# A two-layer graph attention network and expert layer on one core: one more buffer, and the order of the work between the layers

## The reference

```python
x = layernorm(x) -> graph network -> + x;   then layernorm -> expert layer -> + x     # 3125 x 256
def _gat(x, src, dst, W, a_src, a_dst, b, heads, ch, concat):
    h = (x @ W).reshape(n, heads, ch)
    es = (h * a_src).sum(-1); ed = (h * a_dst).sum(-1)
    e = leaky_relu(es[src] + ed[dst], 0.2)
    w = exp(e - segment_max(e, dst)[dst])
    out = segment_sum(h[src] * (w / segment_sum(w, dst)[dst])[:, :, None], dst)
h = _gat(x, ..., heads=4, ch=64, concat=True)      # layer 1
h = relu(_layernorm(h, ln_g, ln_b))
out = _gat(h, ..., heads=1, ch=256, concat=False)  # layer 2
```

## Time and profile before

| | |
|---|---|
| median of 3 runs | 1420.41 us (1419.89 to 1422.87) |
| the profiled execution: its own time, its span | 1427.7 us, 1426.0 us |
| TensorE busy | 1182.3 us, 83% |
| VectorE, ScalarE, GpSimd busy | 858.3, 689.4, 700.6 us (60%, 48%, 49%) |
| mean granted TensorE clock | 0.936 of full speed |
| layer 1, steps | about 84 to 613 us of the span |
| between the layers | about 613 to 640 us |
| layer 2, steps | about 640 to 971 us |
| expert layer | the rest |

### The profile page before, as it was taken

The page is one execution under the profiler, slowest core; times in us unless marked ns, Lnnn a source line. Parts: engine busy times, 40 slices in busy tenths (PEclk is TensorE's granted clock), DMA queues, the critical chain, the costliest instruction groups (busy, mean ns, idle before and its releaser), DMA issues.

```text
span 1426.0 us, 24459 instructions
## 1 busy us (share of the span) xinstructions
PE 1182.3 (83%) x7697; PEld 819.6 (57%) x7698; DVE 858.3 (60%) x2544; ACT 689.4 (48%) x1833; POOL 700.6 (49%) x621
## 2 busy tenths in 40 slices
PE   2765998879888889957787888783799999999997
PEld 1654333334333433435465565552799999999996
DVE  8778988788789778743476765787422222222222
ACT  1567676657566666733333433340534344334432
POOL 1002778557668663017676666630244445454544
PEclk9979999999999999978898998996899999999999
DMA  7023633634643372053445554534033332323221
GB/s 248 1 73 123 168 103 105 181 96 110 168 128 103 108 190 67 27 210 110 151 139 178 168 178 123 181 99 108 12 98 96 94 95 40 92 37 97 35 37 27
DMA packets 137151, 157.04 MB, mean 110 GB/s; under 512 B 58935, under 2 KB 116504, under 8 KB 137064
## 3 DMA queue, kind: packets, MB, share of 16 engines
q0 software_dynamic: 33616, 73.02, 20.9%
q1 hardware_dynamic: 101344, 81.57, 18.6%
q10 hardware_dynamic: 2104, 1.38, 0.3%
HBM read 121.19 MB, written 35.52 MB: 110 GB/s over the span
## 4 chain that ended last, share of the span: by engine, by line
PE 42%; DVE 21%; ACT 9%; issue 9%; another core or an unknown queue 6%; DMA 5%; POOL 5%; ACTq 1%; POOLq 0%; DVEq 0%; SPq 0%
PE bank L1449 11%; PE bank L1457 11%; PE bank L1321 6%; ACT ring_a L1042 5%; PE bank L1400 4%; POOL arena L801 4%; DVE ring_a L1937 3%; DVE ohk L1665 3%; DVE ohs L1661 2%; PE bank L1277 2%; DMA out_x<-ring_a,si 2%; PE bank L1370 1%; DVE st L1546 1%; ACT XE L1006 1%
## 5 line engine op out<-in xcount | busy, mean ns | idle before, releaser
L801 POOL DMA_INDIRECT arena<-rows,idx_e x365 | 405.3, 1110 | 321.0 <-issue 92.2
L1321 PE MATMUL bank<-ring_a,slots 128*65 128x384 f32 (+1 forms) x1000 | 356.6, 465 | 34.2 <-DVE ring_a L1937 28.5
L1042 ACT ACTIVATE ring_a<-vbb,slots 128x384 f32<-128x384 f32 (+1 forms) x500 | 243.8, 562 | 16.2 <-DMA vbb<-v_rows 7.6
L1400 PE MATMUL bank<-h2t,ring_a 128*128 128x257 f32 x700 | 187.9, 412 | 32.8 <-issue 16.8
L1937 DVE SCALAR_TENSOR_TENSOR ring_a<-ring_a,arena 128x1536 f32<-128x1536 f32 (+1 forms) x125 | 192.7, 1543 | 31.2 <-ACT ring_a L1042 23.5
L1150 ACT ACTIVATE ring_a<-bank,cols 128x128 f32<-128x128 f32 x432 | 128.6, 370 | 160.1 <-PE bank L1449 159.6
L1321 PEld LDWEIGHTS bank<-ring_a,slots 128*65 128x65 f32 x1000 | 127.6, 144 | 112.5 <-issue 57.2
L1400 PEld LDWEIGHTS bank<-h2t,ring_a 128*128 128x128 f32 x700 | 136.8, 205 | 68.2 <-issue 25.4
L1449 PEld LDWEIGHTS bank<-ring_a,arena 128*128 128x128 f32 x1056 | 123.1, 192 | 1.7
L1449 PE MATMUL bank<-ring_a,arena 128*128 128x128 f32 x1056 | 123.2, 275 | 0.0
L847 POOL DMA_INDIRECT gs<-gates,gk x54 | 51.2, 949 | 146.2 <-DVE gk L2089 137.6
(11 more groups left out here) (303 smaller groups left out, 1644.5 us busy)
## 6 DMA issues: line engine op xcount, KB each, us to landing
counts_all<-arena SPq DMA_DIRECT2D x14, 800.0 KB
arena<-counts_all SPq DMA_DIRECT2D x14, 800.0 KB
arena<-in_L_ffn_W SPq DMA_DIRECT2D x8, 1024.0 KB, 7.5
vbb<-v_pairs SPq DMA_DIRECT2D x23, 320.0 KB
arena<-rows,idx_e POOLq DMA_INDIRECT x365
XB<-general_sums SPq DMA_DIRECT2D x38, 130.0 KB
vbb<-in_L_ffn_W SPq DMA_DIRECT2D x4, 1024.0 KB
spare<-in_L_ffn_W SPq DMA_DIRECT2D x4, 1024.0 KB
```

Of the source, the lines that this page charges most:

```text
L801: pool.indirect_dma_start(to[:, k, 0:width], None, table, bass.IndirectOffsetOnAxis(idx_e[:, m * PAIR + k:m * PAIR + k + 1], 0)).then_inc( ...
L1042: ins = act.activation(S1[q % SLOTS1][:, h * k * P:(h + 1) * k * P].rearrange("p (t n) -> p t n", n=P), vb1[:, 0:k, h, :], ACT.Copy, scale ...
L1321: pe.matmul(bank[h][0:CH + 1, 0:w_], slots[:, s, h * (CH + 1):(h + 1) * (CH + 1)], S1[q % SLOTS1][:, h * w_:(h + 1) * w_], start=(s == 0), ...
L1400: ins = pe.matmul(bank[(j % 2) * 2 + i][:, 0:W2T], S2[q2 % SLOTS2][:, i * P:(i + 1) * P], h2t[:, s, 0:W2T], start=(s == 0), stop=(s == NT ...
```

## The change

Five edits, made together. (1) `PAIR2` starts at step 8 rather than 3 and ends at 162 rather than 163. The pairs of pairs are then used at steps 11, 19, 26, 34, 41, 49 and so on to 162. (2) The last dense block of layer 1 makes three groups of one tile each, with spreads at 126, 128, 130 and norms at 129, 131, 133 as before; roots at 130, 132, 134, refinements at 131, 133, 135 and turns at 133, 135, 137. (3) Block 0 of layer 1 has a buffer of its own, `vb0`, and `block_rows(1)` goes out ahead of the 25 stores of the first table, with no wait on s_r. (4) `np2` is made by ScalarE instead of VectorE, and VectorE no longer waits for the second layer's exponentials. (5) The spread of layer 2's first scores and its copy (`spread_rows`, `rows_out`) stand ahead of the wait for the flags and the branch, and TensorE's spread waits for the first exponential (s_ex 3) instead of s_vt; ScalarE's wait for s_vt is gone.

```diff
-PAIR2 = [3 + p * 164 // PAIRS2 for p in range(PAIRS2)]
+PAIR2 = [8 + p * 158 // PAIRS2 for p in range(PAIRS2)]
...
-    groups = [Group(range(t0, t0 + k), True, NT * (b + 1)) for b, (t0, k) in enumerate(B1)]
+    groups = [Group(range(t0, t0 + k), True, NT * (b + 1)) for b, (t0, k) in enumerate(B1[:-1])]
+    groups += [Group([B1[-1][0] + i], True, NT * len(B1), 2 * i) for i in range(B1[-1][1])]
...
-        g.spread = [g.end + 1 + 2 * i for i in range(n)] if g.dense else []
+        g.spread = [g.end + 1 + g.late + 2 * i for i in range(n)] if g.dense else []
...
+        vb0 = sb("vb0", [P, B1[0][1], HEADS, P])
...
-                sp.wait_ge(s_r, b * NT)
+                if b > 1:
+                    sp.wait_ge(s_r, b * NT)
...
             half_tile_rows(1)
+            block_rows(1)
             for t in range(NT):
                 sp.wait_ge(s_scl, t + 1)
...
-                if q % NT == 0 and 0 < q // NT < len(B1):
+                if q % NT == 0 and 1 < q // NT < len(B1):
                     block_rows(q // NT)
...
                 act.activation(second, esm, ACT.Exp, scale=power).then_inc(s_ex, 1)
+                if layer:
+                    act.wait_ge(s_ex, 4)
+                    act.activation(np2[:, :, :], p2[:, :, :], ACT.Copy, scale=-1.0).then_inc(s_ex, 1)
...
-                act.activation(vb1[:, t, :, :], bank[7][:, :].rearrange("p (h n) -> p h n", h=HEADS), ACT.Copy).then_inc(s_vbs, 1)
+                act.activation(vb0[:, t, :, :], bank[7][:, :].rearrange("p (h n) -> p h n", h=HEADS), ACT.Copy).then_inc(s_vbs, 1)
...
-                                             vb1[:, 0:k, h, :], ACT.Copy, scale=u1[:, s, h:h + 1])
+                                             (vb1 if b else vb0)[:, 0:k, h, :], ACT.Copy, scale=u1[:, s, h:h + 1])
...
             weights(1, p2, pu2[:, :, :], v2, np2[:, :, :], v2[:, :, :], SLOPE)
+            rows_out(B1[0][1])
             act.wait_ge(s_fl, 2)
...
             act.sem_inc(s_gen, 1)
-            act.wait_ge(s_vt, 2)
...
             extremes(1, 1)
+            pe.wait_ge(s_ex, 3)
+            spread_rows(range(B2[0][0], B2[0][0] + B2[0][1]))
             pe.wait_ge(s_fl, 2)
...
             pe.wait_ge(s_vt, 2)
-            spread_rows(range(B2[0][0], B2[0][0] + B2[0][1]))
...
-                v.wait_ge(s_ex, 2 * layer + 2)
-                if layer:
-                    link(v.tensor_scalar(npv[:, :, :], p[:, :, :], -1.0, None, ALU.mult))
+                if layer == 0:
+                    v.wait_ge(s_ex, 2)
```

More of the change, by code:

```diff
@@ L141, with __init__ @@
 class Group:
-    def __init__(self, tiles, dense, end):
-        self.tiles, self.dense, self.end = list(tiles), dense, end
+    def __init__(self, tiles, dense, end, late=0):
+        self.tiles, self.dense, self.end, self.late = list(tiles), dense, end, late
 def plan1():
-    groups = [Group(range(t0, t0 + k), True, NT * (b + 1)) for b, (t0, k) in enumerate(B1)]
+    groups = [Group(range(t0, t0 + k), True, NT * (b + 1)) for b, (t0, k) in enumerate(B1[:-1])]
+    groups += [Group([B1[-1][0] + i], True, NT * len(B1), 2 * i) for i in range(B1[-1][1])]
     for t in range(NE, NT, 2):
@@ L1064, in _, with rows_out @@
                 q += 1
+            def rows_out(n):
+                act.wait_ge(s_vb, n + 1)
+                what = next((what for q, what in ROWS_AT.items() if ROWS_OF[q] == n), 0)
+                if isinstance(what, str):
+                    k = int(what[-1])
+                    m = len(EDGE_TILES[k * 4:k * 4 + 4]) * P
+                    act.activation(ve2[:, k * 512:k * 512 + m], bank[7][:, 0:m], ACT.Copy).then_inc(s_vbs, 1)
+                else:
+                    m = B2[what][1] * P
+                    act.activation(vb2[what % 2][:, 0:m], bank[7][:, 0:m], ACT.Copy).then_inc(s_vbs, 1)
             weights(1, p2, pu2[:, :, :], v2, np2[:, :, :], v2[:, :, :], SLOPE)
+            rows_out(B1[0][1])
             act.wait_ge(s_fl, 2)
@@ L1092, in hooks2 @@
                     act.activation(xnT[:, e % 4, :, :], bank[6][:, 0:D].rearrange("p (k n) -> p k n", k=2), ACT.Copy).then_inc(s_TS, 1)
-            def rows_out(n):
-                act.wait_ge(s_vb, n + 1)
-                what = next((what for q, what in ROWS_AT.items() if ROWS_OF[q] == n), 0)
-                if isinstance(what, str):
-                    k = int(what[-1])
-                    m = len(EDGE_TILES[k * 4:k * 4 + 4]) * P
-                    act.activation(ve2[:, k * 512:k * 512 + m], bank[7][:, 0:m], ACT.Copy).then_inc(s_vbs, 1)
-                else:
-                    m = B2[what][1] * P
-                    act.activation(vb2[what % 2][:, 0:m], bank[7][:, 0:m], ACT.Copy).then_inc(s_vbs, 1)
             def exponents(p):
@@ L1287, in hooks1 @@
                     for h in range(HEADS):
-                        ins = pe.transpose(bank[6][:, h * (CH + 1):(h + 1) * (CH + 1)], OT[0:CH + 1, h, i * P:(i + 1) * P],
+                        ins = pe.transpose(bank[6][:, h * (CH + 1):(h + 1) * (CH + 1)], OT[0:CH + 1, h, (t - CB[block_of(t)][0]) * P:(t - CB[block_of(t)][0] + 1) * P],
                                            ident[0:CH + 1, 0:CH + 1])
@@ L1334, in _, with spread_rows @@
                 q += 1
+            def spread_rows(tiles):
+                for i, t in enumerate(tiles):
+                    ins = pe.matmul(bank[7][:, i * P:(i + 1) * P], v2[:, t, 0:1].broadcast_to([P, P]), ident[:, :], start=True, stop=True)
+                ins.then_inc(s_vb, 1)
             pe.wait_ge(s_HS, 2 * NT)
@@ L1345, in _ @@
                 general_layer(1, 1, lambda s, h: h2t[:, s, 0:W2T], W2T)
-            def spread_rows(tiles):
-                for i, t in enumerate(tiles):
-                    ins = pe.matmul(bank[7][:, i * P:(i + 1) * P], v2[:, t, 0:1].broadcast_to([P, P]), ident[:, :], start=True, stop=True)
-                ins.then_inc(s_vb, 1)
             def rows_at(q):
@@ L1890, in hooks1 @@
                         X = XB[:, t % 2, ds(bad1, 1), :]
-                        o, s_done = orow[:, i, :], s_on
+                        o, s_done = orow[:, t - CB[block_of(t)][0], :], s_on
                     else:
@@ L1914, in hooks1 @@
                     after(v, s_T, NT + e - 3)
-                    o = orow[:, i, :] if g.dense else orow[:, edge_row(t), :]
+                    o = orow[:, t - CB[block_of(t)][0], :] if g.dense else orow[:, edge_row(t), :]
                     v.tensor_scalar(xn[:, e % 4, :], o, mv[:, t, 0:1], rstd[:, t:t + 1], ALU.subtract, ALU.mult).then_inc(s_xn, 1)
```

1 line of the change is left out of this document (removed).

## The result

The change made the kernel slower. On the chip of the comparison it took 1436.14 us (median of 20 runs, 1427.9 to 1444.6) against 1422.91 us for the kernel before (20 runs, 1417.57 to 1438.76): ratio **1.0084**, 95% interval 1.0066 to 1.0102. I had predicted 1417.2 us, three microseconds faster; the result is outside my range.

What follows compares the result with a forecast made beforehand. No engine was full throughout; layer 2 was taken as nearest to bound by GpSimd's gathers. Terms -4.9 - 0.2 + 0.9 + 1.0 gave -3.2 us, off the median 1420.41 to 1417.2 us, range 1411 to 1423.

Steps and rivals of the forecast that it cites:

- Own buffer, -4.9: Start of layer 1's block 1: ScalarE starts 6.4 us earlier, 1.5 lost waiting for gathers; -4.9 us, bounds -6.4 and -3.2.
- pair 0 ready: Start of block 1: pair 0, wanted at 143.1 us rather than 149.51, would have its gathered data by then.
- the 2.76 us from issue to use: A gather's data is usable 2.76 us after issue; used to put layer 1's pair 1 ready at 148.5 us.
- Rival C: Layer 1: the buffer's gain is waited off at several early pairs; +1.7 us, 1422.1 us; chance 0.13.
- rival E: Layer 1's first ten gathers: one or two slowed by busy VectorE; sum -1.5 us, 1418.9 us; chance 0.12.
- Three groups, -0.2: Between the layers: tiles 10 to 12 normalised singly, last store 0.2 us earlier; bounds -0.5 and +0.8.
- Spread ahead of the branches: Start of layer 2: first step 1.3 us earlier, hidden behind gathers already running, counted only as TensorE's lead.
- Pairs from step 8, +0.9: Layer 2, pairs 4 and 5: product delayed 4.7 us, less 1.3 and two thirds of 3.79 regained; +0.9 us.
- tail, +1.0: End of layer 2: 13 steps instead of 12 behind the last products; +1.18 or 0 if hidden, taken as +1.0 us.
- the gathers come nearest to setting layer 2's length: Layer 2: earlier work counts only if it starts the gathers earlier or shortens what follows the last one.
- 1.18 for the step: Layer 2's end: cost of one dense step, from 12 steps and hooks between 956.72 and 970.89 us.
- Rival D: Layer 2: TensorE late at pairs 4 and 5, product 6.1 us later; sum +2.8 us, 1423.2 us; chance 0.15.

Runs made afterwards that it cites:

- e18: Changed kernel with PAIR2 put back to steps 3 to 163, second time, on another even chip, against the kernel before: 0.9981.
- e17: Kernel before with only PAIR2 changed, to steps 8 to 162, second time, on another even chip: 1.0020.
- e3: Kernel before with only block 0's own score buffer and the early load of block 1, even chip: 1362.51 us, 0.9996.
- e12: Kernel before with own buffer, np2 on ScalarE, early spread, one group as before, and PAIR2 from 3 to 157, even chip: 1.0086.
- e11: Kernel before with only PAIR2 changed, to steps 3 to 157, even chip: 1.0070.
- e2: Changed kernel with PAIR2 put back to steps 3 to 163, even chip, against the kernel before: 1361.43 us, 0.9989.
- e4: Kernel before with only the last block's three groups of one tile, even chip: 1363.85 us, 0.9999.
- e1: Kernel before with only PAIR2 changed, to steps 8 to 162, even chip: 1368.28 us, 1.0034.
- e7: Kernel before with six slots instead of four for layer 2's pairs, pausing chip: 1452.29 us, 1.0104.
- e8: Kernel before with only PAIR2 changed, to steps 13 to 162, pausing chip: 1443.85 us, 1.0061.
- e14: Kernel before with only PAIR2 changed, to steps 8 to 167, pausing chip: 1.0042.
- e13: Kernel before with only PAIR2 changed, to steps 3 to 167, pausing chip: 1.0039.
- e16: Kernel before with only PAIR2 changed, to steps 3 to 162, pausing chip: 1.0017.
- e9: Kernel before, unaltered, run against itself on an even chip: 1.0006.
- e5: Changed kernel, unaltered, against the kernel before on a pausing chip: 1443.54 us, 1.0054.
- e15: Kernel before with own buffer, np2 on ScalarE, early spread, one group as before, and PAIR2 from 3 to 167, pausing chip: 0.9990.

## Why the prediction was wrong

*Own buffer, -4.9.* Right in mechanism. Layer 1's steps end 3.9 us earlier in the recorded pair and 4.0 between e18 and e17; the changed kernel's first dense matmul is 1.4 us later in the recorded pair, so the steps themselves are 5.4 shorter. ScalarE's and VectorE's waits went as worked out. The price was mis-sized: I had pair 0 ready, and it costs 1.69 us beside the 1.06 of pair 1. The reason is the 2.76 us from issue to use, which I took from layer 2: here the fifth gather is issued at 140.77 and its data used at 146.34, 5.57 us, and for pair 1 it is 3.61. All eight kernels with the buffer show both waits, 1.5 to 1.8 and 0.7 to 1.1 us; none of the twelve without it does. Rival C, that the gain is absorbed at early pairs, is seen too: in e3 and e12 VectorE waits another 2.6 and 2.7 us for gathered rows near 212 us, 6.1 in all, and e12's layer 1 is as long as e11's (500.4 and 500.1 us from its first matmul to its last) although block 1 starts 51.7 us behind the first step and not 57.7. In e2 and e18 these waits are under 0.5, and the layer takes 495.6 and 495.5. What decides between the two is open.

*The early gathers beside a busy VectorE (rival E).* I had read no price in the rows, and there is one. The first nine intervals of gathers took 14.15 us against 12.91, with one gather of 2.39. Over all traces it is 13.62 to 14.23 us in the eight kernels with the buffer, where VectorE is busy for 11.3 us or more of them, and 12.86 to 13.00 in the twelve without it, where it is busy for about 6: 0.6 to 1.4 us more. The direction is that of the Trainium skill's rule (SBUF — State Buffer, Who interferes with whom), which says that VectorE in a two-port mode keeps GpSimd out of the shared port. Whether VectorE's instructions here are of that mode, no run shows.

*Three groups, -0.2.* Measured +2.0 from layer 1's end to the first gather in the recorded pair, of which the slow projections are 1.5 (6.05 us against 4.52). The granted clock of the stretch is 0.56 against 0.79. But e4 and e1 give 22.6 alike. The kernel before's 21.9 and e7's 21.7 are the shortest such stretches of all traces; the others take 22.3 to 23.9 with the old groups, and with the new ones 22.3 to 22.7 but for the changed kernel's own 23.9. So the +2.0 is the luck of two executions, most of it in the clock, not the groups' price. Nothing gained, nothing lost.

*Spread ahead of the branches.* TensorE's spread starts with the first gather (632.52 and 632.50), where it came 2.4 us behind it, and the first product of layer 2's dense steps at 636.21, 3.9 us earlier than before. As I had put it, this starts no gather earlier.

*Pairs from step 8, +0.9, and tail, +1.0: this is the step that failed.* I priced edit 1 at 1.9 us in all, as one delay at the pairs 4 and 5, mostly repaid, and one hidden step at the end. Timed alone it costs 4.1 us (e1) and 3.0 (e17) on even chips, and about the same PAIR2 with a start at 13 costs 8.3 on a pausing one (e8). The place was wrong as well. At the pairs 4 and 5 the changed kernel is not late: its product is 3.1 us earlier behind the first gather than before (688.37 and 632.50, against 693.43 and 634.46), and the gather that waits for it 2.0. On even chips the gathers of layer 2 take 276.4 us in e1 and 276.0 in e2 and e4, so nothing is lost on the way, and the tail carries the loss (+2.5 to +3.1). In the recorded pair the gathers carry +5.8, nearly all of it at one stall. And the sentence that the gathers come nearest to setting layer 2's length, on which the whole pricing stood, fails on a pausing chip: with six slots GpSimd was almost 10 us further ahead at the end and the kernel no faster.

*The size of the tail.* It is +1.7 us in the recorded pair. There the last products end 10.4 us behind the last gather, 10.7 before, and the 13 steps behind them take 16.3 us, the 12 before 14.3: the added step lies bare. On even chips it is the other way round: the steps behind the last products take 14.5 us in e1 and 15.0 in e2, and the products come 3 us later, behind TensorE's wait at pair 40. The 2.0 us a step of e11 is therefore not a price that holds at every end. I had 1.18 for the step and nothing for pair 40 in front of VectorE's normalisation.

*Rival D* had the right sign with 1423.2, but not the place: it too put the delay at the pairs 4 and 5. Sum of the recorded pair: -3.9 + 2.0 + 5.8 + 1.7 - 0.1, with rounding +5.4; the medians show 13. On even chips the parts multiply to 1.0023 (e1, e2) and 1.0001 (e17, e18).

**What stays open.** Why the loss is 0.5 to 0.8% on pausing chips and so much smaller on even ones. Single executions there differ by up to 21 us (1417.6 to 1438.8 for the kernel before), so one trace of each kernel can't say how much of the +5.8 is the step list's and how much is where the stalls of the next section fell. That edit 1 alone costs as much as the whole change there was not measured; e8, another late start, did (1.0061). e14 (start 8) and e13 (start 3) are alike at 1.0042 and 1.0039, and the end alone (e16) is not resolved at 1.0017. So the cause of the loss in the comparison itself is open beyond this: PAIR2 alone can make a loss of that size there.

## What to carry to other kernels

When step numbers hang work of different engines together by hand, look at each place where a wait for a transfer and a long piece of unrelated work share an in-order engine: the work belongs ahead of the wait, and a shift of one step can swap the two (here beside 5 us of work). Test whether a suspected bound is one before pricing by it: two more slots moved the last gather further ahead of its product and gained nothing. And when a view is split by tile, add up all its parts: with six slots a third of the gathers writes to another tile, and a reading of one tile alone would put the last gather 15 us too early.

## What the runs showed of the hardware

The chips differ by 4 to 5% for one and the same program: the kernel before took 1363 to 1366 us on three of them and 1425 to 1436 on two, and 1423 on the recorded one. Of its two traces, the recorded one and e9, layer 1's steps end at 612.6 and 585.1 us, layer 2 takes 336.6 and 298.2 from its first gather to its last dense step, and what follows takes 455.0 and 455.6. On the slower ones GpSimd, ScalarE, VectorE and TensorE all have idle time in layer 2 that no instruction explains. The groups of lines in layer 2, of the changed kernel on the recorded chip (632 to 977 us) and of the kernel before on an even one (e9, 607 to 906 us), for GpSimd's gathers and TensorE's dense steps, last the idle time by releaser:

```profile
L805 POOL DMA_INDIRECT arena<-rows,idx_e x210 | 210.2, 1001 | 188.1 <-DMA rows<-h2t 80.9 <-issue 55.8 <-PE bank L1378 36.0
...
L1407 PE MATMUL bank<-h2t,ring_a 128*128 128x257 f32 x700 | 189.6, 418 | 43.0 <-DVE ring_a L2003 22.2 <-issue 20.4
```
```profile
L801 POOL DMA_INDIRECT arena<-rows,idx_e x210 | 209.3, 997 | 144.2 <-DMA rows<-h2t 78.5 <-issue 53.6 <-PE bank L1370 12.0
...
L1400 PE MATMUL bank<-h2t,ring_a 128*128 128x257 f32 x700 | 179.8, 403 | 35.8 <-DVE ring_a L1997 35.7
```

The "issue" part of TensorE's idle time is absent on the even chip. Adding up the idle times marked issue or remote from 636 to 965 us, ScalarE's is 114 us in the kernel before, 138 in the changed one, 149 in e5, 81 in e15, and 0 in e9 and e18. The longest single stall of the recorded trace is the one ahead of the 111th gather. ScalarE, then TensorE:

```profile
799.09 0.38 ACT L1110 ACTIVATE xnT<-bank 128x256 f32<-128x256 f32 x1 [17.00 <-remote]
```
```profile
791.21 3.79 PE L1407 MATMUL bank<-h2t,ring_a 128*128 128x257 f32 x8 [5.73 <-issue]
...
799.52 1.02 PE L1396 MATMUL bank<-wr,xnT 128*128 128x8 f32 x4 [4.52 <-ACT xnT L1110]
```

ScalarE stands 17 us, TensorE waits for it, the product comes at 804.10, and GpSimd's 8.44 us wait at 805.01 is the end of that chain. The gathers also pause after every tenth on these chips, 1.9 to 2.4 us in the median of each trace, against 0.3 on the even ones. That the instruction supply is late is a guess that fits (the Trainium skill, Runtime: NRT & Kernel Launch, Instruction fetch mechanics, says that each engine's instructions come in blocks over a DMA queue, and that this is mostly hidden), but no run here shows it: the page's rows of the two instruction queues read 44 and 43 packets on pausing chips and on two even ones (e1, e18), and 44 and 44 in e9.
